# Moving layer-norm chains, value products, token transposes and VectorE's share in a fused fp32 decoder layer

## The chip, the cores and the metric

The kernel runs on one NeuronCore of a Trainium2 chip. The metric is the device time of one execution in microseconds (us), lower is better. All times below are in us unless marked ns.

## The reference

The input x is (2, 512, 1024) in fp32. Three pre-norm residual stages follow each other: `x = x + attention(layernorm(x))`, `x = x + cross(layernorm(x), ctx)`, `x = x + ffn(layernorm(x))`.

- Attention: 32 query heads on 8 key/value heads of width 32, rotary embedding, causal softmax, output projection.
- Cross: layernorm(x) and a context (2, 1024, 1024) are fake-quantised to 8 bits (`clip(round(x / s + z), 0, 255)`) and multiplied.
- Ffn: `x @ W_org.T` plus a sum over 8 low-rank experts (rank 64), weighted by a softmax of scores that come from the mean of the normed tokens.

## The kernel before, in words

Batch b is 0 or 1. A batch has four token tiles t of 128 rows. fp32 products are made of three matmuls of fp32r parts (high x high, high x low, low x high), so a weight piece (128x512) is fetched by SyncE (`fetch`), copied to a high part on ScalarE (`make_high`, L1054), and its low part is the difference, made by VectorE (L1231) or GpSimd (L1558, `low_piece`). Which engine does it is decided in `on_vector`. Tokens are normed (statistics on VectorE, a chain of ten to thirteen one-column operations that gives 1/sqrt(var), `norm_scale` L816, and one ScalarE operation `normalise`), turned on TensorE by eight transposes of a tile (`turn_tokens` L858), and taken out of PSUM as a high part by ScalarE (`tokens_high` L1133) and a low part by VectorE (`tokens_low` L1307). A norm is named (which, b): which is 1 before attention, 2 before cross, 3 before ffn. `CHAINS_ON_VECTOR` names the norms whose chain runs on VectorE; the other chains run on GpSimd.

Every engine walks the same list of 660 slots (j) in its own program and does in each slot what the planner put there. In slots 0 to 3 TensorE makes v and k of batch 0 for one token tile each (24 steps of three matmuls: 8 of v, 16 of k). Slots 4 to 41 hold the query products of batch 0 and the turning of batch 1. From slot 42 (`first_unit`) 256 units follow, one to a slot: a unit u is the attention of one head and one query tile. It is spread over slots: score in slot u, maximum (VectorE L1251) and exponential (ScalarE L1104) in the same slot, transposes of the probabilities (L917) three slots later, and for each four units the product with the values (`values`, L921) four slots later. After 16 units a group ends: its sums are inverted, spread, turned (`turn_inverse`, slot 4 after its last unit), taken out (5), multiplied (6), split in parts (7), and an `out` step can use it from slot 9 on. Between these, dense steps (three matmuls of 512 columns, or one for cross) fill each slot by a credit in planned time. After the units come slots of one dense step each: the rest of ffn down, out, up, cross and ffn of batch 1.

The planner (`Plan.cut`, L191) goes through the slots with a planned clock `now`. It places a step when `ready` says that what it needs was noted enough slots, and enough planned us, before (`past`, L253). The tables: "hi" and "low" of a weight piece; "round" and "centre" of a context piece, which is quantised in place in its stage buffer by a ScalarE Relu, a VectorE rounding (L1236) and a centring (L1069 or L1241) into its weight slot; a stage buffer is fetched anew one slot after its piece is "done". For norms: "stats", "chain", "apply", then for which=2 "second" (VectorE rounding, L1323) and "third" (ScalarE, L1151), then "turn" and "tokens". For a norm outside the units, turning is placed 1 slot and 1.2 planned us after its source, "apply" or "third".

The order within a slot is written out by hand. VectorE: norm statistics and tokens of the first stage, tokens of the tables, maximum, taking out turned probabilities, rotary parts, low parts, rounding, centring, taking tiles out of PSUM (waits for TensorE), corrections, inverting, scaling, statistics (with a chain, where it is VectorE's), "second". Queues are strictly in order: what waits holds what is behind it. SyncE's start is x tile 0, weight piece 0, identity, piece 1, x tile 1, pieces 2 and 3, x tile 2, a bias, pieces 4 and 5, x tile 3, pieces 6 and 7; piece 4 waits until piece 0 has its low part (four stage buffers), and so on.

```
for j, (first, end) in enumerate(plan.slots):      # TensorE
    if j < NT:
        for half in range(2):
            turn_tokens(1, 0, j, half)             # right before the tile's own 24 steps
...
        if not self.past(j, source, 3 if unit else 1, now, 1.2):   # planner, turning
            continue
```

## Time and profile before

| what | value |
|---|---|
| median of 3 runs | 791.65 us (790.46 to 792.01) |
| the profiled execution's own time | 793.04 us |
| its span | 791.2 us, 12919 instructions |
| TensorE matmuls busy | 693.7 us (88%) |
| VectorE busy | 421.7 us (53%) |
| ScalarE busy | 429.9 us (54%) |
| GpSimd busy | 307.6 us (39%) |
| chain that ended last | TensorE 58%, VectorE 15%, GpSimd 9%, ScalarE 8%, issue 6% |

The span is the execution between its first and last instruction as the profiler has it; 1.8 us lie around it. The table of waits says which instruction ended an idle stretch of an engine.
### The profile page before, as it was taken

The page shows a single profiled execution, that of the slowest core. Times are in us where ns is not written, and L with a number is a line of the kernel's source. Part 1 is how long each engine was busy: PE and PEld are TensorE (multiplying, and loading weights), DVE is VectorE, ACT ScalarE, POOL GpSimd, SP SyncE. Part 2 cuts the span into 40 slices and gives each one's busy share as a digit, 9 for nine tenths or more (in the row PEclk, how much of TensorE's full clock was granted, in tenths as well). Part 3 has the DMA queues.
Part 4 walks back from the last instruction along what each step waited for, and adds up shares of the span by engine and source line. Part 5 has one row for each costly group of instructions (what it writes and reads, how often), then busy time and mean ns, then how long its engine had stood idle before and what let it go on. Part 6 is the DMA issues. An engine that isn't in the chain of part 4 may idle for free.

```text
span 791.2 us, 12919 instructions
## 1 busy us (share of the span) xinstructions
PE 693.7 (88%) x4608; PEld 556.9 (70%) x4608; DVE 421.7 (53%) x1123; ACT 429.9 (54%) x1025; POOL 307.6 (39%) x384
## 2 busy tenths in 40 slices
PE   3999599999999899998768687799996787799998
PEld 3897477788777677875546475588875666588886
DVE  3366377776777536656648353433336569831212
ACT  3325378878787667797665653646314660512320
POOL 5337655543342534471304710505713011525510
PEclk9998899999999999999979698999999797699999
DMA  7504856563445606225350430403425342323102
GB/s 251 193 2 159 245 174 170 157 172 97 136 121 177 201 23 189 64 75 163 112 164 1 130 75 4 120 14 108 160 88 179 100 148 85 120 93 107 41 13 94
DMA packets 43823, 93.49 MB, mean 118 GB/s; under 512 B 5488, under 2 KB 5872, under 8 KB 42224
## 3 DMA queue, kind: packets, MB, share of 16 engines
q1 hardware_dynamic: 40176, 76.94, 30.2%
q0 software_dynamic: 3584, 15.73, 8.3%
q8 instruction: 37, 0.61, 0.3%
q14 instruction: 26, 0.21, 0.1%
HBM read 72.72 MB, written 19.92 MB: 117 GB/s over the span
## 4 chain that ended last, share of the span: by engine, by line
PE 58%; DVE 15%; POOL 9%; ACT 8%; issue 6%; DMA 2%; SPq 1%; DVEq 0%; ACTq 0%
PE dense L1023 37%; PE probt L917 7%; PE score L905 5%; PE pv L932 4%; POOL w_lo L1558 3%; PE score L1023 2%; DVE stats L1295 2%; DVE prob_all L1251 2%; ACT stage L1060 2%; ACT prob_all L1104 2%; POOL ln_s L828 2%; DVE act_t L1318 1%; POOL prob_all L1575 1%; POOL ln_s L830 1%; DVE prob_all L1344 1%
## 5 line engine op out<-in xcount | busy, mean ns | idle before, releaser
L1023 PE MATMUL dense<-w_hi,act_t 128*128 128x512 f32 (+1 forms) x684 | 233.4, 404 | 23.6 <-DVE act_t L1318 10.7
L1251 DVE CUSTOM_DVE_ANT_0 prob_all<-score,mask_sb 128x128 f32<-128x128 f32 (+3 forms) x256 | 123.7, 487 | 141.4 <-PE score L905 139.5
L1558 POOL TENSOR_TENSOR w_lo<-stage,w_hi 128x512 fp32r<-128x512 f32 x89 | 116.4, 1316 | 191.5 <-ACT w_hi L1064 191.2
L1104 ACT ACTIVATE prob_all<-prob_all,neg_max 128x128 f32<-128x128 f32 (+3 forms) x256 | 143.2, 559 | 72.4 <-DVE neg_max L1251 70.6
L1023 PEld LDWEIGHTS dense<-w_hi,act_t 128*128 128x128 f32 x684 | 133.3, 200 | 51.8 <-DVE act_t L1318 11.8
L1023 PE MATMUL dense<-w_lo,act_t 128*128 128x512 f32 (+1 forms) x372 | 138.5, 393 | 5.6 <-DVE xres L1389 3.1
L1023 PE MATMUL dense<-act_t,w_hi 128*128 128x512 f32 x408 | 139.6, 424 | 1.8 <-DVE xres L1367 1.8
L917 PE MATMUL probt<-ident_sb,prob_all 128*128 128x128 f32 x640 | 113.9, 277 | 1.4 <-ACT prob_all L1113 1.1
L905 PE MATMUL score<-k_stack,q_stack 96*128 96x128 f32 (+3 forms) x256 | 92.1, 364 | 13.9 <-DVE neg_max L1251 7.5
L1064 ACT ACTIVATE w_hi<-stage 128x512 fp32r<-128x512 f32 x117 | 71.9, 624 | 50.9 <-PE dense L1023 31.1
L1113 ACT ACTIVATE prob_all<-probt 128x128 f32<-128x128 f32 (+3 forms) x160 | 68.2, 426 | 47.0 <-PE probt L917 46.0
L917 PEld LDWEIGHTS probt<-ident_sb,prob_all 128*128 128x128 f32 x640 | 80.8, 143 | 16.3 <-issue 2.4
L1023 PEld LDWEIGHTS dense<-w_lo,act_t 128*128 128x128 f32 x372 | 74.5, 202 | 16.5 <-DVE w_lo L1241 3.9
L1023 PE MATMUL dense<-act_t,w_lo 128*128 128x512 f32 x204 | 81.9, 401 | 0.0
L1023 PEld LDWEIGHTS dense<-act_t,w_hi 128*128 128x128 f32 x408 | 70.5, 195 | 10.1 <-issue 2.0
L905 PEld LDWEIGHTS score<-k_stack,q_stack 96*128 96x128 f32 x256 | 49.8, 195 | 33.8 <-issue 14.3
L932 PE MATMUL pv<-prob_all,values_sb 128*32 128x128 f32 x1280 | 48.7, 279 | 6.8 <-DVE prob_all L1260 3.5
L932 PEld LDWEIGHTS pv<-prob_all,values_sb 128*32 128x32 f32 x1280 | 31.1, 109 | 27.2 <-issue 13.7
L1260 DVE COPY prob_all<-probt 128x128 f32<-128x128 f32 (+3 forms) x96 | 46.8, 487 | 5.5 <-PE probt L917 5.0
L1023 PE MATMUL dense<-q_stack,act_t 128*128 128x512 f32 x180 | 48.8, 421 | 0.0
L1104 ACT ACTIVATION_READ_ACCUMULATOR prob_all<-prob_all,neg_max 128x1 f32 x256 | 48.6, 190 | 0.0
L1569 POOL TENSOR_TENSOR act_t<-inv_wide,act_t 128x512 fp32r<-128x512 f32 x16 | 20.6, 1286 | 70.4 <-ACT act_t L1131 70.4
(156 smaller groups left out, 916.0 us busy)
## 6 DMA issues: line engine op xcount, KB each, us to landing
q_stack<-rope_dram POOLq DMA_DIRECT2D x16, 768.0 KB, 7.4
stage<-in_w_qk SPq DMA_DIRECT2D x40, 256.0 KB, 3.0
rope_dram<-act_t SPq DMA_DIRECT2D x40, 256.0 KB, 3.3
stage<-in_w_o SPq DMA_DIRECT2D x32, 256.0 KB, 3.0
stage<-in_ctx_kv SPq DMA_DIRECT2D x24, 256.0 KB, 3.1
stage<-in_w_org SPq DMA_DIRECT2D x24, 256.0 KB, 2.8
xres<-in_x SPq DMA_DIRECT2D x8, 512.0 KB, 6.6
prob_all<-in_x SPq DMA_DIRECT2D x8, 512.0 KB, 6.8
```

What stands on the lines that cost most here:

```text
L828: ln(engine.tensor_scalar(tmp, g, g, vh, ALU.mult, ALU.mult))
L905: engine.matmul(score_bank[u % 2][:, 0:length], q_stack[0:TERMS * HD, gi % 2, h, i * P:(i + 1) * P], k_stack[0:TERMS * HD, gi % 2, 0:lengt ...
L917: last = engine.transpose(dst[:, c * P:(c + 1) * P], prob[:, u % P_SLOTS, c * P:(c + 1) * P], ident_sb[:, :])
L932: last = engine.matmul(pv_bank[h * HD:(h + 1) * HD, i * P:(i + 1) * P], values_sb[:, b, c, g * HD:(g + 1) * HD], prob_t[:, (u + h) % PROBT ...
L1023: last = engine.matmul(dst, lhs, rhs, start=(k == 0 and c == 0), stop=(k == g.kts - 1 and c == len(pairs) - 1))
L1064: engine.activation(slot_hi(p, 0, NW), raw, ACT.Copy).then_inc(a_hi, 1)
L1104: engine.activation(prob[:, u % P_SLOTS, 0:length], prob[:, u % P_SLOTS, 0:length], ACT.Exp, bias=neg_max[:, m:m + 1], scale=-1.0, accum_o ...
L1113: engine.activation(prob_t[:, u % PROBT_SLOTS, 0:length], probt_bank[u % 2][:, 0:length], ACT.Copy).then_inc(a_probt, 1)
L1251: engine.tensor_tensor_reduce(prob[:, u % P_SLOTS, 0:length], score_bank[u % 2][:, 0:length], mask_sb[:, S - length:S], -1.0, HIGHEST, ALU ...
L1260: engine.tensor_copy(prob_t[:, u % PROBT_SLOTS, 0:length], probt_bank[u % 2][:, 0:length]).then_inc(v_probt, 1)
L1558: engine.tensor_tensor(slot_lo(p, 0, NW), raw_of(p), slot_hi(p, 0, NW).bitcast(F32), ALU.subtract).then_inc(g_piece, 1)
L1569: engine.tensor_tensor(dst[:, 1, g, :], attn, dst[:, 0, g, :].bitcast(F32), ALU.subtract).then_inc(g_attn, 1)
```

## The change

- `CHAINS_ON_VECTOR` also gets (1, 0): the chains of the first four norms go from GpSimd to VectorE.
- First stage: TensorE turns the next tile in the middle (after 12 of 24 steps) of the tile before it, instead of between two tiles. ScalarE's and VectorE's starting orders are rewritten to suit, and VectorE takes the tokens' low part before the statistics of the tile after. SyncE loads x tiles 2 and 3 after piece 7.
- `PV_LAG` = 5: value products run 5 slots behind instead of 4, and turning, taking out, scaling and splitting a group's result, and the first slot of its `out` step, each one slot later.
- `LATE_TURN_US` = 5.0: outside the units, turning is placed 5.0 planned us after its source instead of 1.2.
- Inside the units the rounding of a context piece is placed one slot later (centring follows it by 2 slots).
- VectorE: maximum and turned probabilities ahead of the tokens in a slot; "second" ahead of the tokens outside the units (inside them it stays last). The low parts of the four odd pieces of the first ffn column block of batch 0 go from GpSimd to VectorE.
- `TOKENS_LAG` = 1 names a number that was there.

No arithmetic is added or left out.

```diff
+PV_LAG = 5
+LATE_TURN_US = 5.0
+TOKENS_LAG = 1
-CHAINS_ON_VECTOR = ((2, 1), (3, 1))
+CHAINS_ON_VECTOR = ((1, 0), (2, 1), (3, 1))
...
-                self.note("round", j, p)
+                self.note("round", j + 1 if unit else j, p)
...
-        return p < 8 and p % 2 == 1 or piece["kind"] == "q" and piece["b"] == 0 and piece["nb"] < 4 or piece["kind"] == "out" and p % 2 == 1
+        return p < 8 and p % 2 == 1 or piece["kind"] == "q" and piece["b"] == 0 and piece["nb"] < 4 or piece["kind"] == "out" and p % 2 == 1 or piece["kind"] == "base" and piece["b"] == 0 and piece["nb"] == 0 and p % 2 == 1
...
-                if not self.past(j, source, 3 if unit else 1, now, 1.2):
+                if not self.past(j, source, 3 if unit else 1, now, 1.2 if unit else LATE_TURN_US):
...
-            return j >= last + 9
+            return j >= last + PV_LAG + 5
...
             fetch(1)
+            fetch(2)
             load_x(0, 1)
-            fetch(2)
             fetch(3)
-            load_x(0, 2)
...
             fetch(5)
-            load_x(0, 3)
             fetch(6)
             fetch(7)
+            load_x(0, 2)
+            load_x(0, 3)
...
-                if j < NT:
+                if j == 0:
                     for half in range(2):
-                        turn_tokens(1, 0, j, half)
+                        turn_tokens(1, 0, 0, half)
...
                 for s in range(first, end):
+                    if j < NT - 1 and s == first + plan.token_steps // 2:
+                        for half in range(2):
+                            turn_tokens(1, 0, j + 1, half)
...
-                if 0 <= u - 4 < UNITS and (u - 4) % GROUP == GROUP - 1:
-                    values((u - 4) // GROUP)
-                for gi in ends_at(u, 4):
+                if 0 <= u - PV_LAG < UNITS and (u - PV_LAG) % GROUP == GROUP - 1:
+                    values((u - PV_LAG) // GROUP)
+                for gi in ends_at(u, PV_LAG):
                     turn_inverse(gi)
...
-            for made in range(4):
+            for made in range(2):
                 make_high(made)
             normalise(1, 0, 0)
+            make_high(2)
             for half in range(2):
                 tokens_high(1, 0, 0, half)
-            for made in range(4, 8):
+            make_high(3)
+            for made in (4, 5):
+                make_high(made)
+            normalise(1, 0, 1)
+            for made in (6, 7):
                 make_high(made)
...
-            for t in range(2):
-                for part in range(2):
-                    norm_stats(1, 0, t, part)
-            for made in (1, 3):
-                low_piece(made)
+            for part in range(2):
+                norm_stats(1, 0, 0, part)
+            low_piece(1)
             for half in range(2):
                 tokens_low(1, 0, 0, half)
+            low_piece(3)
+            for part in range(2):
+                norm_stats(1, 0, 1, part)
...
+                if j < NT - 1:
+                    for half in range(2):
+                        tokens_low(1, 0, j + 1, half)
                 if j < NT - 2:
                     for part in range(2):
                         norm_stats(1, 0, j + 2, part)
-                if j < NT - 1:
-                    for half in range(2):
-                        tokens_low(1, 0, j + 1, half)
...
+                if 0 <= u < UNITS:
+                    maximum(u)
+                if 0 <= u - 3 < UNITS and probt_on[u - 3] == "vector":
+                    take_out_turned(u - 3)
+                if not 0 <= u < UNITS:
+                    for b, t in at["second"].get(j, ()):
+                        quantise_second(b, t)
                 for which, b, t, half in at["tokens"].get(j, ()):
                     tokens_low(which, b, t, half)
```

## Rows read from the trace of the kernel before

**Rows 1.** The page: 40 slices of the span, tenths.
```profile
PE   3999599999999899998768687799996787799998
PEclk9998899999999999999979698999999797699999
```

**Rows 2.** Windows in the units: busy by engine, granted clock, DMA share, GB/s.
```profile
97.30:350.00 252.70, 245.11 (x2098) 196.38 (x2099) 168.66 (x523) 193.56 (x547) 117.94 (x135) 0.99 0.48 139
...
440.00:520.00 80.00, 64.18 (x395) 48.70 (x394) 31.09 (x90) 40.65 (x106) 24.51 (x30) 0.88 0.31 81
```

**Rows 3.** Windows in batch 1's late norms, the same columns.
```profile
598.27:652.10 53.83, 39.71 (x172) 31.50 (x171) 33.74 (x101) 33.05 (x48) 6.26 (x6) 0.84 0.40 128
...
660.46:685.30 24.84, 17.53 (x53) 12.33 (x51) 23.04 (x64) 10.05 (x15) 10.85 (x8) 0.66 0.21 67
685.30:700.00 14.70, 12.80 (x57) 10.56 (x58) 10.22 (x19) 5.95 (x9) 2.08 (x2) 0.88 0.25 85
```

**Rows 4.** Waits of TensorE: us in total, times, longest.
```profile
PE probt L889 <- ACT xnorm L1151: 14.0, 3, 6.2
...
PE dense L1023 <- POOL w_lo L1558: 7.9, 6, 3.5
...
PE probt L889 <- DVE act_t L1318: 6.6, 5, 2.1
PE score L905 <- DMA q_stack<-rope_dram: 6.3, 1, 6.3
...
PE pv L932 <- DVE prob_all L1260: 3.5, 5, 1.1
PE pv L932 <- ACT prob_all L1113: 3.1, 4, 1.6
```

**Rows 5.** The chain that ended last, 10 to 35 us: start, length, what.
```profile
13.95 5.43 PE dense L1023 x24
...
26.57 3.13 PE dense L1023 x24
29.70 5.31 PE score L1023 x48
```

**Rows 6.** Timeline of TensorE up to the first score.
```profile
24.53 1.06 PE L889 MATMUL probt<-ident_sb,xres 128*128 128x128 f32 x8
...
26.57 0.39 PE L1023 MATMUL dense<-w_hi,act_t 128*128 128x256 f32 x1 [0.98 <-DVE act_t L1318]
...
66.09 0.63 PE L889 MATMUL probt<-ident_sb,prob_all 128*128 128x128 f32 x4 [1.72 <-DVE act_t L1318]
...
97.29 0.66 PE L905 MATMUL score<-k_stack,q_stack 96*128 96x128 f32 x2 [6.32 <-DMA q_stack<-rope_dram]
```

**Rows 7.** Timeline: GpSimd's first chain, first and last operation.
```profile
5.85 0.23 POOL L821 TENSOR_SCALAR ln_s<-mean_var 128x1 f32<-128x1 f32 x1 [5.41 <-DVE mean_var L1299]
...
9.18 0.77 POOL L833 TENSOR_SCALAR ln_s<-mean_var,ln_s 128x1 f32<-128x1 f32 x1
```

**Rows 8.** Timeline: a chain on VectorE, first and last operation.
```profile
662.02 0.15 DVE L821 TENSOR_SCALAR ln_s<-mean_var 128x1 f32<-128x1 f32 x1
...
664.13 0.21 DVE L833 TENSOR_SCALAR ln_s<-mean_var,ln_s 128x1 f32<-128x1 f32 x1
```

**Rows 9.** Timeline of GpSimd: start of norm (1, 1)'s four chains, and what follows them.
```profile
49.61 0.21 POOL L821 TENSOR_SCALAR ln_s<-mean_var 128x1 f32<-128x1 f32 x1 [17.06 <-DVE mean_var L1299]
...
66.29 2.54 POOL L1521 TENSOR_TENSOR xres<-xres 128x512 f32<-128x512 f32 x2
```

**Rows 10.** Windows of the scores alone: length, TensorE busy (count), weight loads, clock, DMA.
```profile
97.30:260.00 162.70, 44.48 (x128) 24.39 (x128) 0.99 0.52 151
262.00:270.50 8.50, 2.43 (x7) 1.32 (x7) 1.00 0.97 254
```

**Rows 11.** Timeline of VectorE at the first turning of norm (2, 1).
```profile
606.85 1.29 DVE L1295 BATCH_NORM_STATS2 stats<-prob_all 128x6 f32<-128x512 f32 x2
...
611.38 0.69 DVE L1323 TENSOR_SCALAR xnorm<-xnorm 128x1024 f32<-128x1024 f32 x1
```

**Rows 12.** Timeline of TensorE at the first and second turning of norm (2, 1).
```profile
613.31 1.04 PE L889 MATMUL probt<-identb_sb,xnorm 128*128 128x128 bf16 x8 [6.24 <-ACT xnorm L1151]
625.56 1.03 PE L889 MATMUL probt<-identb_sb,xnorm 128*128 128x128 bf16 x8 [4.58 <-ACT xnorm L1151]
```

More of the change, by code:

```diff
@@ L391, in due_norms @@
                     self.note("turn", j, (which, b, t, half))
-                    self.note("tokens", j + 1 if unit else j, (which, b, t, half))
+                    self.note("tokens", j + TOKENS_LAG if unit else j, (which, b, t, half))
                     halves.append(j)
@@ L1176, in scalar_program @@
                 if j < NT - 1:
-                    normalise(1, 0, j + 1)
+                    if j:
+                        normalise(1, 0, j + 1)
                     for half in range(2):
                         tokens_high(1, 0, j + 1, half)
-                for gi in ends_at(u, 5):
+                for gi in ends_at(u, PV_LAG + 1):
                     take_out_inverse(gi)
@@ L1198, in scalar_program @@
                     spread(gi)
-                for gi in ends_at(u, 7):
+                for gi in ends_at(u, PV_LAG + 3):
                     attn_high(gi)
@@ L1472, in vector_program @@
                         route_mean(b)
-                if 0 <= u < UNITS:
-                    maximum(u)
-                if 0 <= u - 3 < UNITS and probt_on[u - 3] == "vector":
-                    take_out_turned(u - 3)
                 for m, part in rotate_at.get(j, ()):
@@ L1504, in vector_program @@
                     invert(gi)
-                for gi in ends_at(u, 6):
+                for gi in ends_at(u, PV_LAG + 2):
                     scale_values(gi)
@@ L1508, in vector_program @@
                     norm_stats(*half)
-                for b, t in at["second"].get(j, ()):
-                    quantise_second(b, t)
+                if 0 <= u < UNITS:
+                    for b, t in at["second"].get(j, ()):
+                        quantise_second(b, t)
                 for b, t in at["third"].get(j - 1, ()):
@@ L1602, in gpsimd_program @@
                     load_stacks(gi)
-                for gi in ends_at(u, 7):
+                for gi in ends_at(u, PV_LAG + 3):
                     attn_low(gi)
```

## The prediction

> **What bounds the kernel now.** I read the page's slices first. TensorE is full for long stretches and has three weak ones: the start up to about 100 us, roughly 350 to 520 us, and 600 to 690 us; its granted clock is low at the same places [rows 1]. Then windows by stage, to see how weak. From 97.3 to 350 us TensorE is busy 245 of 253 us, so only less TensorE work or a removed stall helps there, and each at full value; from 440 to 520 it is busy 64 of 80 [rows 2]. Then the table of waits, to see which waits a change in order can reach [rows 4]: 14.0 us for ScalarE's quantised tokens (three waits), 7.9 for GpSimd's low parts, 6.6 for VectorE's token parts, 6.3 for the first q_stack, 3.5 and 3.1 for the turned probabilities. The late windows show that a wait costs more than its length: between 598.27 and 652.10 no engine is full (TensorE 39.7, VectorE 33.7, ScalarE 33.1 of 53.8 us), with TensorE's mean clock at 0.84 [rows 3]. That stretch is a loop of waits, not work. Between 660.46 and 685.30 VectorE is busy 23.0 of 24.8 us and is the bound; moving TensorE's transposes cannot help inside it [rows 3].
>
> **The change, part by part.** The sum is made on the profiled execution (span 791.2, own time 793.04, which is 1.4 above the median) and the difference is taken off the median.
>
> *First chain.* On GpSimd it ran from 5.85 to 9.95 us, 4.10 us [rows 7]. The same ten operations on VectorE take 662.02 to 664.34, 2.32 us [rows 8]; the hand-over from VectorE's statistics falls away (about 0.1). ScalarE norms the tile next with nothing new ahead of it, so the first dense matmul comes 1.9 us earlier, at about 12.1 instead of 13.95. GpSimd is then free for piece 0's low part about 4 us sooner, which also releases the fetch of piece 4. Ends: 0.5 (weights late instead of tokens) to 1.9.
>
> *Turning in the middle of a tile.* Tile 1's products start at 26.57, after eight transposes (1.06 us from 24.53) and an idle 0.98 us [rows 6]. The transposes remain, the idle goes, three times (the other two rows show the same 0.97 and 0.98): 2.9 us. What could be late instead is the norm. A tile takes 3.13 + 5.31 = 8.44 us of products [rows 5]; mid-tile is 3.13 + 4 x 0.33 = 4.5 us in. SyncE now issues x tile 2 only after piece 7, which waits for piece 3's low part, at about 14; with the DMA queues full I let it land at 19 to 20. VectorE then needs the token parts of tile 1 (to 21.9), statistics 1.5, a chain 2.3, ScalarE 1.25: ready at 27.2, and mid-tile 1 is at 28.4. 1.2 us of cover; if the load lands 3 us later, about 2 us are lost once. Tile 3 has the same margin or more. Ends: 1 to 2.9. So the first stage ends 1.9 + 2.9 = 4.8, less 0.3 for small hand-over losses: 4.5 us earlier.
>
> *What that does to the first score.* GpSimd starts the four chains of norm (1, 1) at 49.61 and adds the first rotary parts only at 66.29 [rows 9]. They started late since VectorE, in order, sat at the tokens of tile 3 until TensorE turned them at the end of tile 2. Turned mid-tile, the chains start near 42.3 and end near 59, 7.3 us earlier. TensorE itself is 4.5 earlier and loses the 1.72 us wait of 66.09 [rows 6], 6.2 in all, as the chains no longer hold ScalarE and through it VectorE. The first score waits 6.32 us for q_stack [rows 6]; the chain behind it runs through GpSimd, SyncE and TensorE in turn, so it moves by the smaller, **6.2 us**. Ends: 3 (DMA landings take back some) to 9 (the other waits of this stretch vanish too). It persists, as TensorE is full afterwards [rows 2].
>
> *Value products a slot later.* Nine waits, 6.6 us [rows 4]. One more slot gives at least 1.2 us [rows 10], longer than all but one of them; I count 4.0 back, the rest reappears at scores. The probability ring costs nothing: in slot 9 the taking out of unit 6 needs the values of units 0 to 3, which TensorE has done at the end of slot 8, ahead of that unit's own transposes.
>
> *Later slots.* `out` of batch 0 gets its last part one slot later, and rounding a slot later lengthens a stage buffer's round trip. Walking the planner for pieces 64 to 79, a delay is mostly swallowed by the landing time: the second column block is complete two to three slots later. So four more slots without a dense step. Seven such slots took 8.5 us, 1.21 each, against 162.7 / 128 = 1.27 with one [rows 10]; about half of an empty one is unit work that is done anyway: 4 x 0.6 = 2.4 lost. Ends: 0.5 to 10. Against it, VectorE no longer sits in the slot at a ScalarE Relu; the waits of dense steps for centred pieces and of scores in that stretch give back perhaps 2.0.
>
> *Four low parts to VectorE.* The longest wait for a GpSimd low part is 3.5 us [rows 4]; it stands behind the last (3, 0) chain. A piece behind it now comes from VectorE, but the next even one is still GpSimd's: 1.5. *Tokens behind the maximum:* five waits of the first ffn steps for tokens get about 0.5 longer: 2.5 lost. Units in all: 4.0 - 2.4 + 2.0 + 1.5 - 2.5 = **2.6 us** (-4 to 7).
>
> *Turning of norm (2, 1).* Today TensorE arrives at the turn at 607.07 and stands 6.24 us, since VectorE does the next tile's statistics and chain (606.85 to 611.1) before the rounding at 611.38 [rows 11, 12]. With 5.0 planned us instead of 1.2 the turn moves from slot 385 to 391: six steps of 0.68 us go first. The statistics stay ahead of the rounding, so turning still happens at 613.0, but with 1.9 us of standing, and the next tiles are further. The loop is then VectorE and ScalarE: statistics and chain 4.3, second and third 1.9, roundings, centrings and taking out some 3.8, about 10 us a tile where the turns now lie 12.25 us apart [rows 12]. Walking four tiles, the second context sum comes at 640 instead of 650: **10 us**. Ends: 4 (steps go first, but the loop stays) and 17 (VectorE's 33.7 us of work plus 3 as the bound [rows 3]).
>
> *Turning of norm (3, 1).* Of the 6.6 us that transposes wait for token parts [rows 4], 2.3 are in the start and 4.3 here, from 678 to 688. Turning moves into the 16 `up` steps, behind the last statistics; up to 685.30 nothing is gained [rows 3], behind it the waits go and part of the 0.88 clock: **4 us** (0 to 8).
>
> Sum: 6.2 + 2.6 + 10 + 4 = 22.8. 791.65 - 22.8 = **768.9 us** (span about 768.4).
>
> One rule speaks against the mid-tile turning, and a row answers first: the clock is granted in full through the slices from 20 to 50 us, in which eight transposes and a 0.98 us wait stand three times between products [rows 1, 6]. The Trainium skill, TensorE: Matmul & The Clock Gate, section on PE-mode transpose, says that transposes do not count as TensorE being busy in the way products do. By that rule the clock might fall in mid-tile; so far the trace does not bear it out.
>
> **The rivals.**
> 1. *The late loop stays shut.* The walk counts VectorE and ScalarE in planned order; they may hold each other as now (ScalarE's Relu behind the norm, VectorE's rounding behind the Relu), so (2, 1) gives 4 and (3, 1) gives 0. For it: between 598 and 652 both are only 62% busy, so latency rules [rows 3]. Against: TensorE did stand inside that loop. 791.65 - 6.2 - 2.6 - 4 = 778.9.
> 2. *More than the sum.* With short stops TensorE keeps its full clock and VectorE's work is the bound: (2, 1) gives 15, (3, 1) 6, the start 8: 791.65 - 8 - 2.6 - 15 - 6 = 760.
> 3. *The clock falls in mid-tile.* Twelve steps after each turning at half clock: 4 x 0.33 + 8 x 0.33 = 4.0 us become 8.0, three times: 12 lost, 780.9. This is the rule above at work; the full clock in those slices speaks against it.
> 4. *Slower: the context round trip opens.* Place: the 16 context pieces of batch 0 and the 8 ffn pieces behind them in four stage buffers. If each piece's extra slot is not swallowed, up to 24 slots of 1.27 us carry no dense step: 30.5 lost instead of the 1 to 3 that I count, 768.9 + 30.5 - 2.4 = 797. It turns the sign from about 20 such slots on. Against: the landing time covers most in my walk.
> 5. *The change does not do what it says:* turning is late by planned time, but later steps wait for the same tokens, so the stall only moves to them. That is rival 1 carried further: 782.
>
> **How the numbers follow.** Forecast 0.50; rival 1 0.22; rival 2 0.12; rival 3 0.04; rival 4 0.05; rival 5 0.05; near no change by several small losses 0.02. The range takes in rivals 1, 3, 5 and most of 2, and the ends of the terms (low: start 8, units 4, (2, 1) 15, (3, 1) 6.5, 758; high: 3, 0, 4, 0, 785). A measurement of this kernel can tell about 0.2% (1.6 us) from no change: faster by more 0.93, within 0.02, slower by more 0.05.
>
> **What would show it.** In the profile after: the first dense matmul near 12.1 (tokens) and starts of tiles near 23.8, 33.2, 42.6 with no idle ahead; GpSimd's first rotary addition near 59; the first score near 91; the waits of value products near 2 us; the clock full up to 50 us; waits for L1151 near 7 us instead of 14.0, with the turns 10 us apart; waits for L1318 at the late norms gone. The last unit should come about 9 us earlier, the second context sum of batch 1 about 19, the end 23. It would be wrong if turns stayed 12 us apart, if x tile 2 held mid-tile 1, or if more than ten unit slots carried no dense step in the cross stage.

## The result and the profile after the change

| | before | after |
|---|---|---|
| median, same chip | 791.83 us (790.46 to 793.52, 4 runs) | 754.0 us (752.23 to 755.86, 4 runs) |
| span of the profiled execution | 791.2 | 753.5 |
| mean granted clock | 0.944 | 0.961 |
| TensorE / VectorE / ScalarE / GpSimd busy, us | 693.7 / 421.7 / 429.9 / 307.6 | 682.1 / 437.3 / 423.4 / 291.9 |

The ratio is 0.952 with a 95% interval of 0.949 to 0.956. The kernel is 37.8 us faster where 22.8 were forecast, and 754.0 lies below the range (758 to 785).

The page's slices of the kernel after, which answer to [rows 1] (a slice is now 18.8 us instead of 19.8):

```profile
PE   4999699999999899998888687998999696799998
...
PEclk9999799999999999999999799999999897999999
```

In the clock's row the dip at the start is no smaller (the mean from 50 us to the first score is 0.90 before and 0.88 now), that between 350 and 520 us is down to one slice, and of the three low slices behind 600 us (7, 7 and 6 tenths) two are left, at 8 and 7. TensorE's own row still has slices of 8 in the middle. TensorE's waits, which answer to [rows 4]:

```profile
PE probt L892 <- ACT xres L1096: 9.5, 1, 9.5
PE dense L1026 <- POOL w_lo L1575: 8.5, 5, 2.6
PE dense L1026 <- DVE act_t L1330: 5.0, 4, 1.8
PE score L908 <- DMA q_stack<-rope_dram: 4.9, 1, 4.9
PE dense L1026 <- DVE prob_all L1401: 4.8, 2, 3.3
PE probt L892 <- DVE act_t L1330: 4.3, 3, 3.6
...
PE misc L974 <- DVE w_hi L1253: 3.9, 1, 3.9
...
PE probt L892 <- ACT xnorm L1157: 1.3, 1, 1.3
...
PE pv L935 <- DVE inv_wide L1284: 1.2, 2, 1.0
```

ScalarE's quantised tokens held TensorE for 14.0 us and now do for 1.3; a wait of 3.9 for a centred context piece has appeared at the sums of the context (L974). The value products waited 6.6 and now 1.2. But these shorter waits are not where most of the surplus is. I followed the same step through both traces; the third column is how much earlier it starts.

| start of | before | after | earlier |
|---|---|---|---|
| first dense matmul | 13.95 | 12.05 | 1.9 |
| first query step | 59.42 | 53.55 | 5.9 |
| score 0 | 97.29 | 88.29 | 9.0 |
| score 175 | 343.46 | 330.04 | 13.4 |
| score 200 | 406.99 | 383.13 | 23.9 |
| score 225 | 474.84 | 438.89 | 36.0 |
| ffn of batch 0, second column block | 501.75 | 472.71 | 29.0 |
| out of batch 1, second column block, tile 1 | 598.07 | 570.93 | 27.1 |
| second context sum of batch 1 | 650.08 | 613.94 | 36.1 |
| cross of batch 1, second column block | 656.73 | 621.14 | 35.6 |
| first ffn step of batch 1 | 698.99 | 661.22 | 37.8 |

Scores behind the congested stretch aren't a clean mark, since dense work has moved behind units; the second ffn column block is a dense step that stands behind the whole congested stretch, and it says 20.0 us for everything between score 0 and itself. The prediction gave the units 2.6. Of the 37.8, then, some 9 lie ahead of the first score, 20 between it and the second ffn block (1.9 of that is given back by 598), 8.5 at the turning of norm (2, 1), 2.2 at that of (3, 1). The border between the last two is the start of cross's second column block; with the second context sum as the border they are 9.0 and 1.6.

**Where 22.5 us went in 50 units.** Between scores 175 and 225 the kernel before took 131.4 us and the new one takes 108.9. Windows of that stretch (the columns of [rows 2]), before and after:

```profile
343.46:474.84 131.38, 102.55 (x702) 76.45 (x700) 75.98 (x202) 85.30 (x204) 46.06 (x81) 0.90 0.39 108
```
```profile
330.04:438.89 108.85, 90.60 (x673) 67.55 (x671) 77.00 (x201) 82.10 (x202) 44.34 (x79) 0.94 0.44 129
```

VectorE does the same work in both (76 and 77 us) and was 58% busy before; ScalarE's work is nearly the same too (85 and 82 us), 65% busy before. So it was neither's load. TensorE stood idle 28.8 us before and 18.3 now; the rest of the 22.5 is a shorter busy time, with a higher clock and 29 fewer matmuls in the stretch, which are done behind it. The waits of VectorE and ScalarE in the same stretch, which the prediction never read, before:

```profile
ACT prob_all L1104 <- DVE neg_max L1251: 27.1, 25, 3.1
DVE prob_all L1251 <- PE score L905: 23.6, 14, 4.2
DVE stage L1236 <- ACT stage L1060: 23.0, 15, 3.3
```

and after:

```profile
DVE prob_all L1263 <- PE score L908: 15.4, 13, 2.7
ACT prob_all L1110 <- DVE neg_max L1263: 11.1, 10, 1.9
...
DVE stage L1248 <- ACT stage L1066: 10.0, 9, 2.0
```

VectorE stood 23.0 us at the rounding of context pieces (`stage`) until ScalarE's Relu was done, and ScalarE stood 27.1 us at exponentials until VectorE had the maximum. TensorE's own waits for maxima were 6.5 us there; over the whole kernel before their row, which [rows 4] leave out, is

```profile
PE score L905 <- DVE neg_max L1251: 7.5, 9, 1.7
```

Each queue is in order, and each had the thing the other wanted behind the thing it waited for itself. VectorE's timeline shows one turn of this, before:

```profile
396.04 0.29 DVE L1251 CUSTOM_DVE_ANT_0 prob_all<-score,mask_sb 128x128 f32<-128x128 f32 x1
396.25 0.08 DVE L1251 DVE_READ_ACCUMULATOR2_ANT neg_max<- 128x1 f32 x1
398.69 0.43 DVE L1236 TENSOR_SCALAR stage<-stage 128x512 f32<-128x512 f32 x1 [2.35 <-ACT stage L1060]
...
402.12 0.43 DVE L1236 TENSOR_SCALAR stage<-stage 128x512 f32<-128x512 f32 x1 [1.27 <-ACT stage L1060]
```

ScalarE's timeline of the same moments, before:

```profile
396.07 0.40 ACT L1104 ACTIVATE prob_all<-prob_all,neg_max 128x128 f32<-128x128 f32 x1 [2.37 <-DVE neg_max L1251]
...
397.85 0.81 ACT L1060 ACTIVATE stage<-stage,quant_sb,inv_scale 128x512 f32<-128x512 f32 x1
...
400.88 0.40 ACT L1104 ACTIVATE prob_all<-prob_all,neg_max 128x128 f32<-128x128 f32 x1 [1.54 <-DVE neg_max L1251]
```

The exponential waits for the maximum, the Relu at 397.85 stands behind it in ScalarE's queue, with a spread, a taking out of turned probabilities and the next exponential between them, VectorE waits for the Relu (398.69) and can't do the next maximum meanwhile, and so ScalarE's next exponential (400.88) is late again (VectorE also makes two corrections of 0.75 us between the rounding and that maximum). After the change the rounding is met one slot later and finds the Relu done, twice out of three times here; the third wait is 0.74 instead of 2.35 and 1.27:

```profile
374.00 0.08 DVE L1263 DVE_READ_ACCUMULATOR2_ANT neg_max<- 128x1 f32 x1
374.00 0.43 DVE L1248 TENSOR_SCALAR stage<-stage 128x512 f32<-128x512 f32 x1
...
376.06 0.42 DVE L1248 TENSOR_SCALAR stage<-stage 128x512 f32<-128x512 f32 x1
...
377.44 0.43 DVE L1248 TENSOR_SCALAR stage<-stage 128x512 f32<-128x512 f32 x1 [0.74 <-ACT stage L1066]
```

### The profile page after: what moved, and what is told of

The parts are those of the page before. It is cut to its first block, busy times and chain, and to the rows that moved or that the text cites. A ratio compares the mean times of both kernels' runs of the same rounds, so it can differ in the third digit from the quotient of the medians.

```text
span 753.5 us, 12965 instructions
## 1 busy us (share of the span) xinstructions
PE 682.1 (91%) x4608; PEld 546.9 (73%) x4608; DVE 437.3 (58%) x1167; ACT 423.4 (56%) x1025; POOL 291.9 (39%) x340
## 4 chain that ended last, share of the span: by engine, by line
PE 64%; DVE 13%; ACT 8%; POOL 6%; issue 5%; DMA 4%; DVEq 0%; ACTq 0%
PE dense L1026 40%; PE probt L920 7%; PE score L908 5%; PE pv L935 5%; PE score L1026 3%; POOL w_lo L1575 3%; DVE stats L1307 2%; ACT prob_all L1110 2%; PE probt L892 1%; ACT stage L1066 1%; ACT w_hi L1070 1%; DMA stage<-in_w_o 1%; DVE prob_all L1356 1%; PE misc L944 1%; DVE ln_s L831 1%
## 5 line engine op out<-in xcount | busy, mean ns | idle before, releaser
L1026 PE MATMUL dense<-w_hi,act_t 128*128 128x512 f32 (+1 forms) x684 | 229.0, 397 | 18.5 <-POOL w_lo L1575 5.9
L1575 POOL TENSOR_TENSOR w_lo<-stage,w_hi 128x512 fp32r<-128x512 f32 x85 | 111.5, 1319 | 216.3 <-ACT w_hi L1070 216.2
L1026 PEld LDWEIGHTS dense<-w_hi,act_t 128*128 128x128 f32 x684 | 130.6, 196 | 44.6 <-issue 8.0
L1026 PE MATMUL dense<-w_lo,act_t 128*128 128x512 f32 (+1 forms) x372 | 136.6, 388 | 1.6 <-ACT w_lo L1075 1.4
L1026 PEld LDWEIGHTS dense<-w_lo,act_t 128*128 128x128 f32 x372 | 73.4, 198 | 12.5 <-ACT w_lo L1075 2.0
L1026 PEld LDWEIGHTS dense<-act_t,w_lo 128*128 128x128 f32 x204 | 39.5, 194 | 9.1
```

Source lines behind the costliest of these rows:

```text
L1026: last = engine.matmul(dst, lhs, rhs, start=(k == 0 and c == 0), stop=(k == g.kts - 1 and c == len(pairs) - 1))
L1575: engine.tensor_tensor(slot_lo(p, 0, NW), raw_of(p), slot_hi(p, 0, NW).bitcast(F32), ALU.subtract).then_inc(g_piece, 1)
```

## The experiments

Twelve kernels, each timed beside the kernel before on the same chip (medians of 4 runs; before 792.47 in the first group, 791.2 in the second, 791.26 in the third). A gain is always taken from that kernel's own before; the changed kernel gains 37.8.

### One part undone

**u_lag**: values a slot earlier again.

```diff
-PV_LAG = 5
+PV_LAG = 4
```

> The changed kernel with the value products back at 4 slots; all else changed. The changed kernel is at 754.0 us. Theory L (the later value products gave most of the 19 us that the units gained beyond the start): back to 766 or more, score 255 near 517 in place of 505.0. Theory R (the rounding one slot later did it): at most 4 us back, 754 to 758, from the 6.6 us of waits of value products. The prediction's own term would have 758 less the one slot regained, 757.

Measured: 757.77 us, ratio 0.957 (0.953 to 0.960), a gain of 34.7. The lag is worth about 3, with intervals that overlap those of the changed kernel; its size isn't settled closer than about -0.5 to 7. TensorE's waits for its value products are 7.2 us in this kernel and 1.2 in the changed one.

**u_round**: the rounding in the Relu's slot again.

```diff
-                self.note("round", j + 1 if unit else j, p)
+                self.note("round", j, p)
```

> The changed kernel with the rounding of a context piece back in the slot of its ScalarE Relu. Theory R (VectorE stood in that slot at the Relu and held the maxima and with them TensorE): 764 to 770, the stretch between unit 175 and unit 225 (108.9 us in the changed kernel, 131.4 before) back above 120. Theory L: within 2 us of 754. The prediction's term, lost slots against waits about even: 753 to 755.

Measured: 764.43, ratio 0.965 (0.962 to 0.969), a gain of 28.0. One slot of rounding is worth 9.8 us. Units 175 to 225 take 122.6 us instead of 108.9, and VectorE stands at the Relu again, as in the kernel before:

```profile
DVE stage L1248 <- ACT stage L1066: 22.3, 15, 3.3
ACT prob_all L1110 <- DVE neg_max L1263: 20.8, 19, 3.8
```

**u_order**: VectorE's tokens ahead of the maximum again (the three blocks in the old order).

```diff
-                if 0 <= u < UNITS:
-                    maximum(u)
-                if 0 <= u - 3 < UNITS and probt_on[u - 3] == "vector":
-                    take_out_turned(u - 3)
                 if not 0 <= u < UNITS:
...
                     if (which, t, half) == (3, NT - 1, 1):
                         route_mean(b)
+                if 0 <= u < UNITS:
+                    maximum(u)
+                if 0 <= u - 3 < UNITS and probt_on[u - 3] == "vector":
+                    take_out_turned(u - 3)
```

> The changed kernel with VectorE's token parts again ahead of the maximum and the turned probabilities inside a slot. Theory O (tokens ahead of the maximum held the units): 762 or more, all of it between unit 175 and unit 255. Theories L and R: within 2 us of 754. The prediction had this order as a loss of 2.5 us, so undoing it would give 751.5.

Measured: 752.09, ratio 0.949 (0.944 to 0.953), a gain of 40.4. This part of the change isn't what helps; undone, the kernel is the same or 2.6 us faster. The intervals of the ratios overlap.

**u_base**: all low parts of the first ffn column block on GpSimd again (the last clause of `on_vector` removed).

```diff
-        or piece["kind"] == "base" and piece["b"] == 0 and piece["nb"] == 0 and p % 2 == 1
```

> The changed kernel with all low parts of the first ffn column block of batch 0 back on GpSimd. Prediction's term: 1.5 us back, 755.5, with a wait of the first ffn steps for a GpSimd low part of 3 to 4 us. If this part gave more, 760 or more, in the first ffn block alone.

Measured: 761.37, ratio 0.961 (0.958 to 0.965), a gain of 31.1: four low parts are worth 6.7 us.

### One part alone, in the kernel before

**a_start**: the first stage alone (chains of (1, 0) on VectorE, mid-tile turning, the starting orders, the x loads); the rest as before.

```diff
-CHAINS_ON_VECTOR = ((2, 1), (3, 1))
+CHAINS_ON_VECTOR = ((1, 0), (2, 1), (3, 1))
...
+                    if j < NT - 1 and s == first + plan.token_steps // 2:
+                        for half in range(2):
+                            turn_tokens(1, 0, j + 1, half)
...
```

> The kernel before with the first stage's part alone: first chains on VectorE, turning in mid-tile, SyncE's and the starting orders. The prediction's term: 6.2 us, about 786. By the changed kernel's trace (score 0 came 9.0 us sooner): 9 to 10 us, about 782. The late units' stalls are not touched, so nothing more should be gained behind score 0 (up to 2.5 us by chance of planning in the units' first half).

Measured: 783.35, ratio 0.989 (0.987 to 0.992), a gain of 7.9. The first score comes 8.8 us earlier and score 127 still 8.9; between scores 127 and 150 it goes back to 6.1. A lead of the start isn't kept in full through the units while the value products stay at 4 slots: from score 127 to 150 a_start takes 40.5 us and u_lag 40.2, the kernel before 37.7 and the changed kernel 36.4.

**a_round**: the later rounding alone.

```diff
-                self.note("round", j, p)
+                self.note("round", j + 1 if unit else j, p)
```

> The kernel before with the later rounding alone. Theory R: VectorE's wait for the ScalarE Relu in the units (23.0 us of standing between units 175 and 225 before) falls to about half, 8 to 12 us faster, 780 to 784. If the order of the maximum and the tokens is needed beside it, 5 us or less.

Measured: 778.74, ratio 0.984 (0.981 to 0.986), a gain of 12.5. It is the largest single part. Up to score 175 it gives 1.0, from there to score 200 another 11.2, to score 225 another 8.5. Of these 20.7 us 13.9 are left at the second ffn column block, as dense steps have moved behind the units. Between scores 175 and 225 VectorE's waits for the Relu are down to 9.2 us and ScalarE's for the maximum to 11.7.

**a_base**: the four odd low parts on VectorE alone.

```diff
+        or piece["kind"] == "base" and piece["b"] == 0 and piece["nb"] == 0 and p % 2 == 1
```

> The kernel before with the four odd low parts of the first ffn column block on VectorE alone. If the part's worth in the changed kernel (7.4 us) is its own: about 784 to 786, gained between the start of base0.0 and of base0.1. If it depends on the later rounding: 790. The prediction's term was 1.5 us.

Measured: 785.07, ratio 0.992 (0.990 to 0.994), a gain of 6.1. Up to the first ffn step nothing differs (438.07 and 438.08); four token tiles on it is 8.6 ahead. GpSimd's timeline in the kernel before shows what the first steps stood behind:

```profile
445.12 0.26 POOL L833 TENSOR_SCALAR ln_s<-mean_var,ln_s 128x1 f32<-128x1 f32 x1
445.33 2.50 POOL L1558 TENSOR_TENSOR w_lo<-stage,w_hi 128x512 fp32r<-128x512 f32 x2
451.35 1.27 POOL L1558 TENSOR_TENSOR w_lo<-stage,w_hi 128x512 fp32r<-128x512 f32 x1 [3.51 <-ACT w_hi L1064]
452.58 1.29 POOL L1569 TENSOR_TENSOR act_t<-inv_wide,act_t 128x512 fp32r<-128x512 f32 x1
453.82 2.52 POOL L1558 TENSOR_TENSOR w_lo<-stage,w_hi 128x512 fp32r<-128x512 f32 x2
```

and TensorE's, in the kernel before, what each cost:

```profile
446.65 0.79 PE L1023 MATMUL dense<-w_hi,act_t 128*128 128x512 f32 x1 [3.50 <-POOL w_lo L1558]
455.15 0.51 PE L1023 MATMUL dense<-w_hi,act_t 128*128 128x512 f32 x1 [1.50 <-POOL w_lo L1558]
```

The two low parts behind the chain are those of pieces 83 and 84, and the wait of 3.50 us is for piece 83, which is odd and first of the two. In a_base VectorE makes it; TensorE does that step at 442.32 without a wait, and the first wait is 2.13 us, for piece 84:

```profile
445.97 0.50 PE L1023 MATMUL dense<-w_hi,act_t 128*128 128x512 f32 x1 [2.13 <-POOL w_lo L1558]
```

The second wait, for piece 86, hardly moves (1.50 and 1.45). Over the stretch from the end of cross to the second ffn column block (415.28 us to 501.75 before, to 493.17 in a_base) TensorE does the same 441 matmuls; it is idle 3.8 us less, of which its waits for low parts make 0.9 (5.0 to 4.1) and those for tokens 2.4 (7.1 to 4.7), and busy 4.8 us less, with the mean clock at 0.91 instead of 0.86. VectorE's waits for scores shrink from 31.6 to 21.9 us.

**a_late2**: later turning outside the units, with "second" ahead of the tokens there.

```diff
-                if not self.past(j, source, 3 if unit else 1, now, 1.2):
+                if not self.past(j, source, 3 if unit else 1, now, 1.2 if unit else 5.0):
...
+                if not 0 <= u < UNITS:
+                    for b, t in at["second"].get(j, ()):
+                        quantise_second(b, t)
...
```

> The kernel before with the later turning of batch 1's norms and the earlier VectorE rounding of the normed tokens outside the units. The prediction's terms: 10 us for norm (2, 1) and 4 for norm (3, 1), 778. The changed kernel's trace had 8.1 and 1.5: 782. Rival 1 of the prediction: 788. Units unchanged.

Measured: 780.04, ratio 0.985 (0.982 to 0.988), a gain of 11.2. At the first `up` step it is 14.7 ahead; of that 9.3 are left at cross's second column block, 8.8 at the next `up` block, and 11.1 at the first ffn step.

The four parts alone sum to 7.9 + 12.5 + 6.1 + 11.2 = 37.7, and the whole gives 37.8. That the two agree so closely is partly luck: the whole also has the value lag (3.1 by u_lag) and the order of the maximum (-2.6 by u_order), which no kernel has alone, and the rounding is worth 12.5 alone and 9.8 undone.

### Why the rounding matters

It could be one of two things. The planner's note also delays centring and the dense steps behind it, so the gain could come from dense steps that are placed later and then find their operands; or it comes from where VectorE stands. Two kernels take these apart.

**p_plan**: the changed kernel's plan, with the rounding emitted by VectorE in the Relu's slot.

```diff
-                for p in at["round"].get(j, ()):
+                for p in (q for q in at["hi"].get(j, ()) if kinds[q] == "cross"):
                     if round_on[p] == "vector":
```

> The changed kernel, but VectorE's rounding stands in its program again in the slot of ScalarE's Relu, while the planner goes on counting it one slot later; the dense steps keep the changed kernel's places. Theory 1 (VectorE standing at the Relu is what was cured; 754.0 changed, 764.4 with the rounding back in planner and program): the old place brings the standing back although the plan is the new one: 762 to 767, VectorE's waits for the Relu between units 175 and 225 near 20 us as against 10.0. Theory 2 (the gain comes from the plan, which puts dense steps later, when their operands are there): 753 to 756, waits of VectorE up, but TensorE's not.

Measured: 767.39, ratio 0.971 (0.968 to 0.975), a gain of 23.9. Its waits between scores 175 and 225 (328.72 to 449.03):

```profile
DVE stage L1248 <- ACT stage L1066: 23.0, 15, 3.3
ACT prob_all L1110 <- DVE neg_max L1263: 22.0, 24, 1.9
```

**p_place**: the old plan (as in u_round), with the rounding emitted one slot later in VectorE's program.

```diff
-                for p in at["round"].get(j, ()):
+                for p in at["round"].get(j - 1, []) * (u > 0 and u <= UNITS) + at["round"].get(j, []) * (u < 0 or u >= UNITS):
                     if round_on[p] == "vector":
```

> The counterpart: the planner counts the rounding in the Relu's slot as before the change, and only VectorE's program has it one slot later. Theory 1: near the changed kernel, 752 to 757, VectorE's waits for the Relu near 10 us. Theory 2: near the kernel with the rounding back, 762 to 766.

Measured: 754.84, ratio 0.954 (0.951 to 0.957), a gain of 36.4. Its waits in the same units (329.44 to 441.97):

```profile
ACT prob_all L1110 <- DVE neg_max L1263: 10.7, 7, 3.2
DVE stage L1248 <- ACT stage L1066: 7.6, 8, 1.5
```

Units 175 to 200 show it most plainly: 63.5 us before, 60.3 in u_round and 62.7 in p_plan, against 53.4 in p_place and 53.1 in the changed kernel. Over the whole kernel the place is worth 8.4 us with the old plan (u_round to p_place) and 13.9 with the new one (p_plan to the changed kernel). The place in VectorE's program is the cause. The plan alone shows no gain: with the rounding at its old place the kernel with the new plan is some 4 us slower than that with the old one (gains of 23.9 and 28.0, intervals that just touch) and just above theory 1's range; with the rounding at its new place it is 1.4 us faster, which isn't beyond the uncertainty. Units 200 to 225 alone don't separate the two: 62.3 us in u_round, 57.7 in p_plan, 59.1 in p_place, 55.8 in the changed kernel. By score 225 p_plan is 2.3 us quicker through the 50 units than u_round, and at the second ffn column block it is 3.0 us behind it.

### The late turning, and one step further

**u_late**: the changed kernel with `LATE_TURN_US` 1.2.

```diff
-LATE_TURN_US = 5.0
+LATE_TURN_US = 1.2
```

> The changed kernel with turning outside the units planned 1.2 us after its source instead of 5.0. Theory 1 (late turning is worth nearly its gain alone, 11.2 us with the order of second): 762 to 766, with TensorE again standing some 10 us in all at ScalarE's quantised tokens instead of 1.3. Rival (in the changed kernel the units leave earlier and the order of second does most of it): 756 to 760.

Measured: 760.88, ratio 0.962 (0.958 to 0.965), a gain of 30.4, so the planned time itself is worth 7.4. It fell between the two theories, nearer to the rival's. The earlier "second", which stays in this kernel, may have the rest of the 11.2; no run has it alone. TensorE's first wait is the old one again:

```profile
PE probt L892 <- ACT xnorm L1157: 12.8, 4, 5.4
```

From tile 1 of the second column block of batch 1's `out` to cross's second column block, u_late wins 2.7 us over the kernel before, the changed kernel 8.5.

**x_base2**: u_order with the odd low parts of the second ffn column block on VectorE too.

```diff
-        or piece["kind"] == "base" and piece["b"] == 0 and piece["nb"] == 0 and p % 2 == 1
+        or piece["kind"] == "base" and piece["b"] == 0 and p % 2 == 1
```

> The changed kernel with VectorE's tokens ahead of the maximum again (that alone ran at 752.1) and the odd low parts of the second ffn column block of batch 0 moved from GpSimd to VectorE as well. If GpSimd's low parts still hold TensorE there (8.5 us of waits for them are left in the changed kernel): 748 to 751. If those waits lie elsewhere, or VectorE is now late for its own work: 752 to 755.

Measured: 754.86, ratio 0.955 (0.952 to 0.958), a gain of 36.4. No further gain: against u_order it is 2.8 us slower on the medians, within overlapping intervals. In that block TensorE's waits for GpSimd's low parts do fall, from 2.5 us in u_order to 0.4, but at the `down` pieces behind it they rise from 2.6 to 6.7:

```profile
PE dense L1026 <- POOL w_lo L1575: 11.5, 8, 2.6
```

That is the row of x_base2 for the whole kernel; u_order has 8.2 in 7 waits. So the waits moved one block on. No version was found that beats the changed kernel beyond the uncertainty.

## Why the prediction was wrong, point by point

**Sign and mechanism of most parts right, the units' term wrong.** The sum had 6.2 + 2.6 + 10 + 4 = 22.8; the trace has 9.0 + about 18 + 8.5 + 2.2 = 37.8, where 18 is the 20.0 between the first score and the second ffn block less the 1.9 given back by tile 1 of `out`. The step that failed is the one sentence "VectorE no longer sits in the slot at a ScalarE Relu; [...] give back perhaps 2.0". It measured 9.8 undone and 12.5 alone. The four low parts, put at 1.5, are the second mis-sized term, with 6.7 and 6.1. The parts undone one by one, 9.8 + 6.7 + 3.1 - 2.6 = 17.0, cover nearly all of the 18, though each is taken at the end of the kernel and not in the units alone. The reason for the error is in how it was priced: the 2.0 was set by TensorE's waits and worked out from no row, and this standing hardly shows there (6.5 us of waits for maxima in the stretch); the window of 440 to 520 us with TensorE busy 64 of 80 [rows 2] was read as a fact and not asked why. VectorE's own waits had 23.0 us under one name in that stretch.

**Value lag** (4.0 back, 2.4 lost in empty slots): 3.1 by u_lag, against 1.6 net; the waits of value products went from 6.6 to 1.2. The empty slots' price is not visible anywhere, and one reason is that they hardly opened: by the planner of the two kernels 50 of the 256 unit slots carry no dense step before and 51 now, 9 and 11 of them between the first cross step and the first ffn step, where I had four more. What the planner does is spread the steps thinner: counted from the first unit, the first ffn step of batch 0 comes 5 slots later (217 instead of 212), the first `down` step 7 and batch 1's first `out` step 11, and all of them come earlier in time. Of the 11 slots 9 go back with the rounding (u_round) and 2 with the value lag (u_lag). That such a slot is cheap since VectorE and ScalarE set its length is argued, not shown.

**Four low parts** (1.5): 6.7 undone, 6.1 alone. I counted what was left of one wait; in the trace of a_base the waits for low parts give only 0.9 us, those for tokens 2.4, and TensorE's shorter busy time at the higher clock 4.8 (of 8.6 gained by the second ffn column block, 6.1 at the end). Which of these brings about the others isn't settled.

**Tokens behind the maximum** (2.5 lost): undoing it gave a kernel 1.9 us below the changed one on the medians, which agrees in sign and isn't beyond the uncertainty.

**Start** (6.2): 9.0 in the trace, 8.8 alone at the first score, 7.9 at the end. First dense 12.05 (12.1 forecast), tiles at 23.72, 32.81, 41.89 (23.8, 33.2, 42.6), TensorE without an idle gap ahead of them, GpSimd's first rotary addition at 57.56 (59), score 0 at 88.29 (91). The tiles came 0.3 us faster each than I had: between the products around it a mid-tile turning takes 0.82 us (from one step's start to the next 1.16 instead of 0.34), less than the 1.06 of its row. The other surplus is the clock: TensorE came to the query products colder before. Windows from the keys' matmuls of 8 columns to the point where the steps run at full clock, before and after:

```profile
55.49:63.43 7.94, 7.94 (x36) 6.89 (x36) 4.44 (x8) 4.12 (x6) 6.11 (x20) 0.58 0.22 69
```
```profile
50.13:55.00 4.87, 4.87 (x30) 4.40 (x29) 4.70 (x8) 3.49 (x6) 3.90 (x11) 0.69 0.12 21
```

Before, three query steps took 1.28 to 1.45 us each, against 0.69 at the full level; now one does. I had said that the first score moves by the smaller of two chains, GpSimd's 7.3 and TensorE's 6.2; it moved by as much as GpSimd's first rotary addition, 66.29 [rows 9] to 57.56, that is 8.7, and TensorE's side came 8.85 earlier (its ninth query step starts at 69.66 and at 60.81). The chain that ended last ran through GpSimd's four chains before and runs through TensorE's query products now:

```profile
57.86 2.77 PE dense L1026 x12
```

**Turning of (2, 1)** (10): 8.5. The loop did not tighten as in my walk: from the first turn to the fourth it took 33.5 us before and takes 32.5 now, nearly 11 apart instead of the 10 forecast. The 12.25 us that I started from [rows 12] was the first of three gaps (12.3, 13.4 and 7.8); now they are 17.0, 6.2 and 9.3. What changed is that TensorE no longer stands in it:

```profile
585.34 0.62 PE L892 MATMUL probt<-identb_sb,xnorm 128*128 128x128 bf16 x8 [1.32 <-ACT xnorm L1157]
...
594.52 1.53 PE L974 MATMUL misc<-w_hi,ones_r 128*128 128x512 f32 x3 [3.92 <-DVE w_hi L1253]
...
602.37 0.62 PE L892 MATMUL probt<-identb_sb,xnorm 128*128 128x128 bf16 x8
608.53 0.62 PE L892 MATMUL probt<-identb_sb,xnorm 128*128 128x128 bf16 x8
...
617.87 0.62 PE L892 MATMUL probt<-identb_sb,xnorm 128*128 128x128 bf16 x8
```

From tile 1 of `out`'s second column block to cross's second column block it does the same 193 matmuls in 50.2 us instead of 58.7. Of the 12.7 us of waits for quantised tokens that went, part came back: the sums of the context now wait 3.9 us for a centred piece of VectorE's and 1.3 for ScalarE's, where they waited 0.8 before (rival 5, in part).

**Turning of (3, 1)** (4): 2.2. From cross's second column block to the first ffn step it takes 40.08 instead of 42.26 us; VectorE does 35.0 us of work there, and at one turn TensorE still stands 3.56. VectorE was busy 87% of it, near the bound that [rows 3] had, and I let the waits behind it vanish too easily.

**The rivals.** Rival 1 (the late loop stays shut) half fell: (3, 1) is near it, (2, 1) isn't. Rival 2 (more than the sum, 760) had the right side for the wrong place: it put 21 us into the late turnings, which gave 10.7, and left the units at 2.6. Rival 3 fell: the steps of k behind a mid-tile turning take 0.33 to 0.34 us from start to start, as those ahead of it do. The window from 10 to 50 us, after:

```profile
10.00:50.00 40.00, 39.35 (x318) 38.98 (x317) 26.66 (x69) 13.27 (x19) 10.16 (x27) 1.00 0.43 155
```

The granted clock of 1.00 there isn't the whole story: the first eight steps of tile 0 take 0.64 us or more each in both kernels, against 0.36 in the later tiles, so I read the level behind the turnings from the steps' lengths.

The Trainium skill, TensorE: Matmul & The Clock Gate, section on PE-mode transpose, says that transposes don't count as TensorE being busy in the way products do. By that rule the clock might have fallen in mid-tile, and this trace doesn't bear it out.

Rival 4 (the context round trip opens, 797) fell: of the up to 24 slots without a dense step that it feared, two opened in the cross stage.

## What to carry to other kernels

Read the waits of every engine in a congested stretch, not only those of the busiest one: here two engines stood 23.0 and 27.1 us for each other in small pieces, in 50 slots of 2.6 us, and TensorE's own waits showed 6.5 us of it. Where an in-order engine takes over another's result within the same slot, try placing the taking over one slot later in its program, without touching the plan; here it was the largest single part. And price a moved low part or rounding by what stands behind it in both queues, not by the one wait that it ends.

## What the runs showed of the hardware

- Eight transposes in the middle of 24 steps leave the clock at its full level (the steps behind them take 0.33 to 0.34 us, as ahead of them), and their row is 1.06 us long there as between tiles [rows 6].
- The granted clock of the records reads 1.00 from the start, while the first eight steps of tile 0 take 0.64 us or more each, against 0.36 in later tiles, and the eight transposes ahead of them 1.94, against 1.06 later and 1.89 behind the keys, where the clock reads 0.50. So TensorE seems to start at the low level without the records showing it.
- The keys' 16 matmuls of 8 columns and eight transposes behind them ran into the low level in both kernels (clock 0.58 and 0.69 in the windows above), though TensorE shows no idle time in these windows or in the 5 us ahead of them.
